# Attention under an adjacency mask on one core: 16 of 128 key blocks per batch turned by VectorE and DMA instead of TensorE

## The reference

```python
h = jnp.maximum(_layernorm(x, axis=-1), 0.0)
q = (h @ Wq + bq).reshape(b, n, H, HD)          # k and v alike
scores = jnp.einsum('bihd,bjhd->bhij', q, k) / jnp.sqrt(jnp.float32(HD))
scores = scores + jnp.where(adj == 0, -1e9, 0.0)[None, None, :, :]
weights = jax.nn.softmax(scores, axis=-1)
out = jnp.einsum('bhij,bjhd->bihd', weights, v)
x = x + out.reshape(b, n, H * HD)
```

## Time and profile before

| | us |
|---|---|
| median of 3 runs | 3952.41 |
| lowest, highest | 3952.12, 3953.52 |
| profiled execution, own time | 3952.87 |
| its span | 3951.1 |
| busy: PE, DVE, ACT, POOL | 3925.2, 3109.3, 3010.7, 1389.6 |

### The profile page before, as it was taken

The page is one execution under the profiler, slowest core; times in us unless marked ns, Lnnn a source line. Parts: engine busy times, 40 slices in busy tenths (PEclk is TensorE's granted clock), DMA queues, the critical chain, the costliest instruction groups (busy, mean ns, idle before and its releaser), DMA issues.

```text
span 3951.1 us, 64302 instructions
## 1 busy us (share of the span) xinstructions
PE 3925.2 (99%) x21504; PEld 3219.8 (81%) x21504; DVE 3109.3 (79%) x5263; ACT 3010.7 (76%) x5386; POOL 1389.6 (35%) x1399
## 2 busy tenths in 40 slices
PE   8999999999999999999999999999999999999998
PEld 7888888888888888888888888888888888888887
DVE  7878878788787887878878788787887868878687
ACT  6877868778686886868868688686886868868687
POOL 4334333343333333333333333333333333334322
PEclk9999999999999999999999999999999999999999
DMA  6233333333323333334233342332433324324232
GB/s 208 60 88 72 88 78 67 85 79 80 83 66 83 89 70 84 73 75 95 63 84 80 68 96 65 82 84 62 96 73 75 87 61 94 80 67 90 51 76 49
DMA packets 722325, 316.44 MB, mean 80 GB/s; under 512 B 629840, under 2 KB 629840, under 8 KB 713424
## 3 DMA queue, kind: packets, MB, share of 16 engines
q1 hardware_dynamic: 722000, 312.34, 34.7%
HBM read 173.28 MB, written 38.27 MB: 54 GB/s over the span
## 4 chain that ended last, share of the span: by engine, by line
PE 92%; DVE 6%; issue 1%; ACT 1%; POOL 0%; DMA 0%; ACTq 0%; POOLq 0%; DVEq 0%
PE T L604 21%; PE misc L558 16%; PE S L589 11%; PE O L623 11%; PE S L590 11%; PE O L616 11%; PE misc L571 9%; DVE pT L909 2%; DVE S L903 1%; PE misc L537 1%; DVE bn L869 1%; DVE qB L886 1%; DVE y L928 0%; DVE qA L886 0%; ACT pT L722 0%
## 5 line engine op out<-in xcount | busy, mean ns | idle before, releaser
L909 DVE TENSOR_TENSOR pT<-T,pT 128x512 fp32r<-128x512 f32 x2048 | 1378.7, 686 | 657.1 <-ACT pT L722 651.5
L722 ACT CAST pT<-T 128x512 fp32r<-128x512 f32 x2048 | 1187.1, 590 | 412.8 <-PE T L604 326.1
L903 DVE CUSTOM_DVE_ANT_0 S<-S,mask 128x1024 f32<-128x1024 f32 x1024 | 1251.9, 1223 | 1.2 <-PE S L590 1.2
L604 PEld LDWEIGHTS T<-ident,probs 128*128 128x128 f32 x8192 | 996.9, 140 | 301.8 <-DVE pT L909 64.4
L604 PE MATMUL T<-ident,probs 128*128 128x128 f32 x8192 | 1236.5, 273 | 4.6 <-DVE pT L909 0.5
L741 ACT ACTIVATE probs<-S,negmax 128x1024 f32<-128x1024 f32 x1024 | 1150.7, 1124 | 7.0 <-DVE negmax L903 3.8
L623 PE MATMUL O<-pT,vs 128*64 128x512 f32 x2048 | 954.5, 466 | 0.2 <-DVE pT L909 0.2
L616 PE MATMUL O<-pT,vs 128*128 128x512 f32 x2048 | 816.1, 398 | 0.0
L558 PE MATMUL misc<-hT,wqk 128*128 128x512 f32 x3036 | 734.3, 391 | 0.0
L456 POOL TENSOR_TENSOR outs<-outs,oT 64x512 f32<-64x512 f32 x255 | 338.2, 1326 | 1024.4 <-DMA outs<-oT 1021.1
L558 PEld LDWEIGHTS misc<-hT,wqk 128*128 128x128 f32 x3036 | 570.0, 188 | 122.0 <-issue 0.2
(11 more groups left out here) (78 smaller groups left out, 3298.9 us busy)
## 6 DMA issues: line engine op xcount, KB each, us to landing
wqk<-wqk_split SPq DMA_DIRECT2D x63, 1024.0 KB, 6.0
xln<-in_x SPq DMA_DIRECT2D x240, 256.0 KB, 2.7
kA<-kA SPq DMA_DIRECT2D x128, 256.0 KB, 3.2
kB<-kB SPq DMA_DIRECT2D x128, 256.0 KB, 3.8
outs<-in_x SPq DMA_DIRECT2D x256, 128.0 KB, 3.6
outs<-oT SPq DMA_DIRECT2D x256, 128.0 KB, 3.6
out<-outs SPq DMA_DIRECT2D x252, 128.0 KB, 3.3
rinv_sq<-rinv_turned SPq DMA_DIRECT2D x512, 2.0 KB, 1.7
```

The source lines that it names most:

```text
L604: mm = pe.transpose(T[:, u % 2, i * P:(i + 1) * P], probs[:, (GB * g + i) % RING, j * P:(j + 1) * P], ident[:])
L722: act.copy(pT[:, u % PT, 0, :], T[:, u % 2, :]).then_inc(p_hi, 1)
L903: dve.tensor_tensor_reduce(S[:, s % 2, :], S[:, s % 2, :], mask[:, s % NB, :], 1.0, 3.0e38, ALU.add, ALU.min, negmax[:, s % RING:s % RING ...
L909: dve.tensor_tensor(pT[:, u % PT, 1, :], T[:, u % 2, :], pT[:, u % PT, 0, :].bitcast(F32), ALU.subtract).then_inc(p_lo, 1)
```

## The change

The table `PACKS` names eight packs of two blocks in each batch (four in the last batch): a pair (at, slot) means that blocks slot and slot + 1 are not turned by PE, and that their turning starts on DVE in step `at`, four steps earlier. Slots 130 and 131 are blocks 2 and 3 of the next batch. The blocks per batch are 10, 11, 42, 43, 74, 75, 77, 78, 106, 107, 109, 110, 125, 126 and 2, 3 of the next.

For a pack, DVE turns the 32x32 squares of 128 x 1024 of `probs` into a scratch area (`turn_pack`). SP stores this to DRAM with four DMAs of 32 partitions (`store_pack`, each 256 pieces of 512 B), waits until they have landed, and loads it back with two DMAs of 128 partitions (`load_pack`, 256 KB each) over the block's own place in `probs`, each square now in its row of squares. ACT and DVE then read `probs` instead of T. In these steps ACT does exponential ahead of probs_hi. The scratch lies over half of the high part of `wv`, which is stored to DRAM once and loaded again in step 110 of every batch but the last; the two last packs use `xln`.

```diff
+PACKS = ((6, 10), (38, 42), (70, 74), (73, 77), (102, 106), (105, 109), (121, 125), (126, 130))
+TWO = 2
+WV_AT = 110
...
+            def store_pack(b, k, at):
+                n, src = len(PACKS) * b + k, squares(at)
+                sp.wait_ge(sq_turned, n + 1)
...
+                for a in range(QUADS):
+                    dst = turned_dram[n % 2, :, :, a, :].rearrange("j c n -> c j n")
+                    sp.dma_start(dst, src[a * SQ:(a + 1) * SQ]).then_inc(sq_out, 16)
+            def load_pack(b, k, slot):
+                n = len(PACKS) * b + k
+                sp.wait_ge(sq_out, 16 * QUADS * (n + 1))
+                for i in range(TWO):
+                    src = turned_dram[n % 2, QUADS * i:QUADS * (i + 1)].rearrange("q c a n -> (q c) a n")
+                    sp.dma_start(probs_of(UNITS * b + slot + i), src).then_inc(sq_in[i], 16)
...
+                    for k, at, slot in packs_of(b):
+                        if u == at:
+                            store_pack(b, k, at)
+                        if u == at + 1:
+                            load_pack(b, k, slot)
+                    if u == WV_AT and not last:
+                        load_wv(b)
...
             def turn_probs(b, u):
+                if pack_of(b, u):
+                    return
...
             def probs_hi(b, u):
+                moved = pack_of(b, u)
+                if moved:
+                    act.wait_ge(sq_in[moved[1]], 16 * (moved[0] + 1))
+                else:
+                    act.wait_ge(turned, turned_to(n))
...
-                    probs_hi(b, u)
+                    moved = pack_of(b, u)
+                    if not moved:
+                        probs_hi(b, u)
                     s = u // 2 + LEAD - 1
                     if u % 2 == 0 and s < SBLOCKS:
                         exponential(b, s)
...
+                    if moved:
+                        probs_hi(b, u)
...
+            def turn_pack(b, k, at, slot):
+                n, pack = UNITS * b + slot, len(PACKS) * b + k
+                dve.wait_ge(exped, GB * (n // NB + 1))
...
+                dve.transpose(squares(at).rearrange("p j (t r) -> p t j r", r=SQ),
+                              probs_of(n, TWO).rearrange("p t (j c) -> p t j c", c=SQ)).then_inc(sq_turned, 1)
```

More of the change, by code:

```diff
@@ L89, with packs_of, pack_of, turned_to @@
 SPREAD_0 = (2, 2, 6, 6, 6, 6, 8, 8)
+PACKS = ((6, 10), (38, 42), (70, 74), (73, 77), (102, 106), (105, 109), (121, 125), (126, 130))
+TWO = 2
+WV_AT = 110
 W_ORDER = ((1, 0), (0, 0), (0, 1), (0, 2), (0, 3), (1, 1), (1, 2), (1, 3))
 XLN_USES = [len(range(r, NB, XLN)) for r in range(XLN)]
+def packs_of(b):
+    return [(k, at, slot) for k, (at, slot) in enumerate(PACKS)
+            if b < B - 1 or at < (PAIRS - 1) * PER]
+def pack_of(b, u):
+    for k, at, slot in packs_of(b):
+        if slot <= u < slot + TWO:
+            return len(PACKS) * b + k, u - slot
+    if b > 0:
+        for k, at, slot in packs_of(b - 1):
+            if slot <= u + UNITS < slot + TWO:
+                return len(PACKS) * (b - 1) + k, u + UNITS - slot
+    return None
+MOVED = [[u for u in range(UNITS) if pack_of(b, u)] for b in range(B)]
+def turned_to(n):
+    b, u = divmod(n, UNITS)
+    return n + 1 - sum(len(MOVED[i]) for i in range(b)) - len([s for s in MOVED[b] if s <= u])
 def some(n):
@@ L205, in qk_buffers, with probs_of, squares @@
             return qB[:, pair % 2, :], kB[:, pair % 2, :, :]
+        def probs_of(n, blocks=1):
+            g, j = n // NB, n % NB
+            at = GB * g % RING
+            return probs[:, at:at + GB, j * P:(j + blocks) * P]
+        wv_shared = wv[:, 0, 0:2, :].rearrange("p c n -> p (c n)").bitcast(F32)
+        def squares(at):
+            return wv_squares[:] if at < V_FROM else xln[:].rearrange("p t (j n) -> p (t j) n", n=P)
         def x_tile(b, t):
@@ L727, in exponential @@
                 if some(free):
-                    act.wait_ge(turned, free)
+                    act.wait_ge(turned, turned_to(free - 1))
+                    moved = [m for m in range(free - NB, free) if pack_of(*divmod(m, UNITS))]
+                    if moved and s % GB == 0:
+                        act.wait_ge(p_lo, moved[-1] + 1)
                 if n == 0:
@@ L1014, in body @@
                         turn_out(b, u // PER - 1, OUT_AT.index(u % PER))
+                    for k, at, slot in packs_of(b):
+                        if u == at:
+                            turn_pack(b, k, at, slot)
                     if u in STATS_AT and not last:
```

49 lines of the change are left out of this document (41 added, 8 removed).

## The result

| | before | after |
|---|---|---|
| median, us | 3952.38 (3952.12 to 3953.52) | 4059.93 (4055.36 to 4064.53) |
| profiled execution, own time | 3952.87 | 4064.53 |
| its span | 3951.1 | 4062.7 |
| its granted TensorE clock | 0.999 | 0.991 |

The changed kernel is slower: ratio 1.0272, 95% interval 1.0254 to 1.0289, which is +107.5 us. The forecast was 4024 us, +71. The losses stand where it put them, in the packs of the four pairs of heads; the time is 36 us longer than it said.

A forecast was written before the change was run, and what follows sets the result against it. PE, busy 99% of the span, was taken as the bound. Losses in the pairs less the v region's gain gave +4.47 us for each of 15 batches and +4.06 for the last: +71 on 3952.9, so 4024 us, range 3925 to 4105.

The forecast's parts named there:

- Step 5: Packs (6, 10), (38, 42): DVE's gapless work behind block 10 makes PE's turns of blocks 15 and 16 1.14 us later.
- step 3: Packs (6, 10), (38, 42): ACT, exponential first, asks for block 10 at 1059.65, cast by 1060.25; DMA and ACT late together.
- Pairs 2 and 3 lose by their second pack: Packs (73, 77), (105, 109): late DMA, then the exponential queued behind the wait; pairs later by 1.78 and 2.17 us.
- The transposition: DVE's turning of a pack's 128x1024 squares: 1.42 us, with twice this as upper end.
- The four stores: Issuing a pack's four stores takes 2.70 us, the last starting 2.0 us after the first.
- The plain leg: From squares turned to first block back through memory: 7.6 us, ends 7.1 and 9.5.
- step 2: Packs (6, 10), (38, 42): first block back at 1052.1 + 7.6 = 1059.7.
- rival C: Leg of 9.5 us or a transposition of twice the time: about +190, 4143 us; chance 0.18 with what lies between.
- the v fills, -1.76: Packs (121, 125), (126, 130): legs hidden beside long fills, all four turns count, -1.76 us a batch.
- A: Rival: legs partly hidden, DVE's stretch in steps 10 to 16 has slack; -20 us, 3933 us; chance 0.18.
- B: Rival: everything hidden, the whole 109 us of turns come off PE, 3844 us; chance 0.06.
- D: Rival: nearly a draw, pairs lose what the v region gives, 3945 to 3960 us; chance 0.05 within 0.2%.

The follow-up runs named there:

- stats_short: The changed kernel with the layer norm statistics of steps 11, 13, 43 and 45 taken over 8 of 512 columns; 4034.74 us, ratio 1.0206.
- second_pack_gone: The changed kernel without packs (73, 77) and (105, 109), six packs left; 3990.65 us, ratio 1.0097.
- loads_alone: The changed kernel with first-half copy_k in step 13 and, in steps 7 and 39, pack loads issued ahead of load_xln; 4037.5 us, ratio 1.0215.
- v_only: The changed kernel with only packs (121, 125) and (126, 130), beside the v fills; 3934.56 us, ratio 0.9954.

## Why the prediction was right or wrong

**Right: the mechanism and the sign.** The waits of the packs in pairs 0 to 3 moved work onto the critical path as forecast, and the v fills won.

- Step 5 of packs (6, 10) and (38, 42), DVE's gapless chain at +1.14 us: where the leg is on time the trace has 0.77 + 0.37 = 1.14, and stats_short took most of it away. In these cases the load landed up to 0.4 us before ACT asked for it, so the two were late nearly together, as step 3 had it.
- Pairs 2 and 3 lose by their second pack: second_pack_gone brought both to about nothing. The sizes, +1.78 and +2.17 against +1.80 and +2.35, agree in part by luck. The leg was shorter than taken, and blocks 78 and 110 were contracted 0.95 and 1.39 us late, not 1.78 and 2.17. A further 0.9 us in pair 2 and 0.5 us in pair 3 came by blocks 80 and 112; the rows there have turns of PE that wait for DVE's probs_low, and how they add up was not worked out. The rest in pair 3 is the clock, below.
- The transposition: 1.24 us, taken as 1.42. The four stores: 1.85 us of issue, taken as 2.70.
- The plain leg: 6.7 to 7.2 us in most cases where nothing is in the way (median 7.0), taken as 7.6. The estimate of about 7 us by the fixed 2.0 us for each DMA, which the page "DMA: Bandwidth & Descriptors" of the Trainium skill states for DMAs issued over GpSimd (section "Anatomy of one DMA"), agrees with these legs, issued by SP.

**Wrong: step 2 of packs (6, 10) and (38, 42).** "First block back at 1052.1 + 7.6 = 1059.7" treated the leg as one number in every batch and kept its upper end, 9.5 us, for rival C alone, as if the leg were long everywhere or nowhere. It is long in 9 of 32 cases at these two packs, 9.4 to 10.6 us. There the load of x and two copies of k share the DMA engines with the pack's load; without them the leg stayed under 9 us (loads_alone), and why it is long in some batches only is open. What the forecast counted of copy_k was only that it comes later itself. These two terms, forecast at +1.14 each, measured +2.32 and +2.36: 2 x 1.2 x 15 = 36 us too little. loads_alone brought them to +1.33 and +1.24.

**Wrong, smaller: the v fills, -1.76.** No leg holds PE up there, but two of the four turns stand between fills that wait for the one bank `misc` (0.4 us), and ACT's order costs 0.2 us at block 130. Measured -1.17: the v fills win 0.59 x 15 = 9 us less than forecast. With 3 us from pairs 2 and 3 that is 48 us above the forecast by the table, which holds the twelve middle batches. By all of them (first +5.9, the next fourteen +7.33 on average, last +3.6) the profiled execution is 112 us longer than before and the forecast 40 us short; the median of the runs lies 4.6 us below that execution.

**Not in the sum: TensorE's clock.** It fell to half (0.50 in the last section, 1.2 of 2.4 GHz) around waits of PE such as the 3.3 us above. The mean of 0.991 bounds what it can have cost at 0.9% of the span, 36 us, if PE had been at work all that time; of 252 whole q and k fills, seven took 3.5 to 4.1 us in place of 2.90, 7 us in all. The stretches tell more. In pair 3 the clock over blocks 100 to 116 was 0.95 in five of 15 batches, which lost 2.9 to 3.15 us, and 1.00 in the ten others, which lost 1.93 on average: 1.1 us a case. In pairs 0 and 1 legs of 10.4 to 10.6 us cost 3.8 us at 0.95 (three cases), and legs of 10.2 to 10.6 us cost 4.8 to 5.2 at 0.90 (four cases): 1.2 us a case. That is an estimate of some 10 us of the 112, and 0.4 to 0.5 us a batch of pair 3's +2.35.

**Left out, and small: DVE against POOL.** The mean of the subtraction with both inputs in SBUF is 742 ns against 685 for the one that reads PSUM: 14 us of DVE's time over 248 blocks. Of these, 16 took 1.2 to 1.7 us, all beside a POOL instruction; 63 others beside one, and all that were beside none, took 0.69. The row at 1259.38 above, 1.46 us, is such a case in v_only. The page "SBUF — State Buffer" of the Trainium skill (section "Who interferes with whom") states that a DVE instruction with two SBUF inputs contends with a GpSimd instruction that reads SBUF, and the 16 fit it.

**The rivals.** A and B asked for short or harmless legs everywhere; the legs ran to 10.6 us. C's leg of 9.5 us did occur, but in 9 of the 32 cases of two packs and not in all. D's balance did not come, since the pairs lost over seven times what the v fills gave.

**The choice that the forecast did not question** was ACT's order. It saw that "ACT has to make the exponential after the fill in any case, which alone is 0.7 us of wait", and took this as a property of the packs. It was one of the code: with the cast first the 0.7 us came back in pairs 2 and 3.

## What to carry to other kernels

A round trip through memory has a distribution, not a duration: look at each place for what else is on the DMA queue or the engines within its few microseconds, and give a long case its own chance. A wait on an engine costs what is queued behind it in order, so take the waiting instruction's position (ACT's cast, SP's load) as a part of the change. And move work off the bound only where the engine that takes it has a gap before the next hand-over: four packs in such places won 45 us, eight lost 107.

## What the runs showed of the hardware

- The first load of a pack, 256 KB in 512 B pieces, landed after 3.0 to 3.4 us in most cases without other large transfers near it. With three other transfers of 256 KB issued within 2.4 us around it, it landed after 3.1 to 4.5 us in 21 cases and 5.0 to 6.3 us in 9 (packs (6, 10) and (38, 42), batches 0 to 14); the DMA engines were busy for 0.93 of the time in the case shown.
- The granted clock of TensorE was at full for most of the time that PE idled and came down about as it went back to work. A wait of 3.3 us was followed by some 7 us at half clock, in which a fill of 12 matmuls took 4.11 us instead of 2.90. In pairs 0 and 1 of after it fell in the nine cases in which PE had waited 2.1 to 3.3 us for block 10 or 42, and in none of those with up to 1.5 us. In pair 3 it fell at two waits of under 1 us each, 2.1 us apart, in batch 4. The same two waits, 0.8 to 1.8 and 0.96 us, stand in all 15 batches, and it fell in five, so they do not decide it alone. The rows are those two contractions and scores behind them, which stand 0.42 us apart instead of the usual 0.23:

```profile
1267.27 0.50 PE L710 MATMUL O<-pT,vs 128*128 128x512 f32 x1 [0.94 <-ACT pT L821]
...
1269.40 0.80 PE L710 MATMUL O<-pT,vs 128*128 128x512 f32 x1 [0.96 <-ACT pT L821]
...
1271.28 0.63 PE L678 MATMUL S<-kB,qB 128*128 128x512 f32 x1
...
1271.70 0.63 PE L679 MATMUL S<-kB,qB 128*128 128x512 f32 x1
```

The window from 1270 to 1272 us shows the lower level, 0.50 (columns as above):

```profile
1270.00:1272.00 2.00, 2.00 (x8) 1.81 (x7) 2.00 (x5) 1.47 (x3) 1.85 (x2) 0.50 0.00 0
```

- DVE turns a 128 x 1024 fp32 tile in 32x32 squares in 1.24 us, with strided order, against 0.71 us for 128 x 512.
